# Layer one's short convolution by pairs of heads: interleaved rows in one product, the odd rows placed by a transfer

## The reference, cut to what matters

```python
avg = cumsum(x, axis=1) / arange(1, l + 1)          # l = 1024 tokens, 256 features = 16 heads of 16
ci = avg per head                                   # (b * H, l, 16)
w = softmax(stt_energy + sigmoid(gate) * dyn)       # 31 weights per token and head, from ci @ W_pe
out[t] = sum over kk of w[t, kk] * padded[t + kk]   # a causal window of 31 tokens
v = out (all heads side by side) @ W_fc.T + residual
v = layernorm(v) * gamma + beta
```

## Time and profile before

| | |
|---|---|
| median of 3 runs | 3462.36 us (3459.31 to 3465.0) |
| the profiled execution's own time | 3466.14 us |
| its span, first to last instruction | 3464.3 us |
| mean granted TensorE clock | 0.979 of full speed |
| instructions | 67597 |

### The profile page before, as it was taken

One profiled execution on the slowest core, in us unless ns is written; L12 is line 12 of the kernel. 1 busy time (PEld: TensorE's weight loads), 2 busy tenths in 40 slices (PEclk: granted clock), 3 DMA queues, 4 the chain that ended last, 5 costly groups with the idle time before them and its releaser, 6 DMA issues.

```text
span 3464.3 us, 67597 instructions
## 1 busy us (share of the span) xinstructions
PE 3307.4 (95%) x25168; PEld 2785.4 (80%) x25168; DVE 2606.8 (75%) x6172; ACT 2076.2 (60%) x4055; POOL 1269.7 (37%) x1073
## 2 busy tenths in 40 slices
PE   7999999999996999999999469999999999999999
PEld 4888888888885799999999347888888888888888
DVE  5877887788777865555554578888888888888884
ACT  4677777777765555655665345555555555555554
POOL 1333333332331366666665332333333332322320
PEclk8999999999998999999999689999999999999999
DMA  5332233222212344444444465555655555655541
GB/s 180 102 114 90 93 114 108 80 64 80 75 45 80 87 115 103 96 104 109 105 97 86 86 132 113 113 127 127 129 125 127 120 123 126 130 125 128 128 102 41
DMA packets 746021, 366.38 MB, mean 106 GB/s; under 512 B 551278, under 2 KB 696246, under 8 KB 745558
## 3 DMA queue, kind: packets, MB, share of 16 engines
q1 hardware_dynamic: 717278, 319.57, 36.4%
q0 software_dynamic: 28416, 42.49, 6.6%
HBM read 224.93 MB, written 135.99 MB: 104 GB/s over the span
## 4 chain that ended last, share of the span: by engine, by line
PE 87%; DVE 6%; ACT 2%; DMA 2%; issue 1%; SPq 1%; POOL 1%; POOLq 0%; DVEq 0%; ACTq 0%
PE bank L2294 10%; PE bank L853 10%; PE bank L1612 10%; PE bank L2308 10%; PE bank L1596 10%; PE bank L833 10%; PE bank L2265 7%; PE bank L130 5%; PE bank L810 3%; PE bank L2244 3%; PE bank L2276 3%; PE bank L2239 1%; ACT sides L1140 1%; PE bank L818 1%; PE bank L846 1%
## 5 line engine op out<-in xcount | busy, mean ns | idle before, releaser
L1492 DVE TENSOR_TENSOR hidden_low<-bank,hidden_high 128x512 fp32r<-128x512 f32 x256 | 176.2, 689 | 263.0 <-ACT hidden_high L1193 262.8
L609 ACT ACTIVATE bank<-bank,b 128x512 f32<-128x512 f32 x256 | 172.7, 675 | 282.2 <-PE bank L833 281.9
L1186 ACT ACTIVATE bank<-bank,fc_bias 128x512 f32<-128x512 f32 x256 | 169.5, 662 | 263.5 <-PE bank L1596 263.5
L853 PE MATMUL bank<-w_high,gT_low 128*128 128x256 f32 x1024 | 309.8, 303 | 2.9 <-DVE gT_low L725 2.9
L2052 ACT ACTIVATE bank<-bank,l_b 128x512 f32<-128x512 f32 x256 | 168.9, 660 | 238.8 <-PE bank L2294 238.8
L2308 PE MATMUL bank<-l_w_high,l_hidden_low 128*128 128x256 f32 x1024 | 307.6, 300 | 0.0
L2265 PE MATMUL bank<-bandT,window 128*32 128x96 f32 x5632 | 271.2, 345 | 22.4 <-DMA bandT<-bands 20.2
L853 PE MATMUL bank<-w_low,gT_high 128*128 128x256 f32 x1024 | 289.4, 283 | 0.0
L853 PE MATMUL bank<-w_high,gT_high 128*128 128x256 f32 x1024 | 289.4, 283 | 0.0
L2308 PE MATMUL bank<-l_w_low,l_hidden_high 128*128 128x256 f32 x1024 | 286.0, 279 | 0.0
L2308 PE MATMUL bank<-l_w_high,l_hidden_high 128*128 128x256 f32 x1024 | 285.5, 279 | 0.0
(11 more groups left out here) (372 smaller groups left out, 10709.3 us busy)
## 6 DMA issues: line engine op xcount, KB each, us to landing
bandT<-bands SPq DMA_DIRECT2D x352, 240.0 KB, 3.7
fc_full<-in_L_ffn_fc_wT SPq DMA_DIRECT2D x32, 1024.0 KB, 5.5
bands<-zeros SPq DMA_DIRECT2D x22, 768.0 KB, 8.6
x<-in_L_attn_x SPq DMA_DIRECT2D x32, 512.0 KB, 6.3
moe_output<-zeros SPq DMA_DIRECT2D x32, 512.0 KB, 7.1
x_after_retention<-x SPq DMA_DIRECT2D x32, 512.0 KB, 2.9
moe_input_and_gates<-xn SPq DMA_DIRECT2D x32, 512.0 KB, 7.7
moe<-moe_output SPq DMA_DIRECT2D x32, 512.0 KB, 7.4
```

What stands on the lines that cost most here:

```text
L609: e.activation(bank[:, :], bank[:, :], ACT.Gelu_apprx_tanh, bias=t.b1[:, f:f + 1]).then_inc(s("g_full"), 1)
L853: m = pe.matmul(out, x, w, start=False, stop=f == KF - 1 and j == 2 and c % 2 == 1)
L1492: v.tensor_tensor(t.hidden.low[:, n % SLICES, :], K.banks[t.bank["expand", i, f, 0]][:, :], t.hidden.high[:, n % SLICES, :], ALU.subtract) ...
```

## The change

The bank of a tile now holds the product of each pair's 32 rows with both heads' bands. `window` has no zeros: row 2d of a pair is feature d of the even head, row 2d + 1 that of the odd head. The moving operand is `bandT[:, :, first:first + 2]`, for each token the weights of both heads, which lie side by side; the matmul has 192 columns, token by token, even and odd. Of the result, an even row is wanted at even columns and an odd row at odd ones. ScalarE makes two copies: the odd columns into a new tile `odd` (all rows), and the even columns into `convT` (all rows). Then a DMA issued on ScalarE's queue writes the 64 odd rows of `odd` over the odd rows of `convT`. `mix` waits for these transfers. The rows of `W_fc` are permuted on the host to match. GpSimd's two memsets of `window` go. `PLACES_D`, `STARTS_D` and `BANKS_D` have new numbers throughout and a new step `place_odd`; the length of a batch stays 16 slots.

```diff
 EARLIER = {...,
+           "odd_placed0": ("x_in0", 256), "odd_placed1": ("x_in1", 256)}
...
 PLACES_D = {
-    "kernel_product": (10.8, 12.8, 14.85, 16.8, 18.8, 20.8, 22.79, 24.8), "gated": (10.8, 12.8, 14.61, 16.8, 18.82, 20.8, 22.8, 24.8),
-    "energies": (11.61, 13.56, 15.61, 17.61, 19.47, 21.61, 23.61, 24.94),
-    "add_in": (6.08, 13.95), "l1_low": 1.03,
-    "convolve": (16.82, 18.13, 19.59, 21.03, 22.48, 23.93, 25.38, 26.83, 28.28, 29.73, 31.18),
-    "mix": (19.06, 20.4, 21.9, 24.8, 26.2, 27.7, 30.6, 31.43),
+    "kernel_product": (10.78, 12.89, 14.88, 16.78, 18.79, 20.83, 22.75, 24.72),
+    "gated": (10.69, 12.36, 14.84, 16.4, 18.61, 20.87, 22.64, 24.58),
+    "energies": (11.36, 13.53, 15.74, 17.77, 19.27, 21.4, 23.55, 25.44),
+    "add_in": (5.06, 13.12), "l1_low": 1.09,
+    "convolve": (16.97, 18.07, 19.67, 21.03, 22.22, 23.95, 25.02, 26.9, 28.62, 29.73, 31.18),
+    "place_odd": (17.09, 18.19, 19.9, 21.15, 22.42, 24.02, 25.25, 27.02, 28.74, 29.85, 31.3),
+    "mix": (19.15, 20.61, 22.1, 24.89, 26.55, 27.9, 31.19, 32.35),
...
-    t.window = K.ring(ctx, "window", 2, [P, H // 2, 2, 2 * t.HD])
+    t.window = K.ring(ctx, "window", 2, [P, H // 2, 2 * t.HD])
+    t.odd = K.ring(ctx, "odd_heads", 2, [P, KD, TT])
...
-            e.memset(t.window[0][:, :, :, :], 0.0)
-            e.memset(t.window[1][:, :, :, :], 0.0).then_inc(s("pool_setup"), 1)
...
         elif name == "window_turn":
-            out = bass.AP(all_of.tensor, all_of.offset, [all_of.ap[0], [4 * t.HD, H // 2], [3 * t.HD, 2], [1, t.HD]])
-            e.copy(out, src).then_inc(s("window"), 1)
+            e.copy(t.window[n % 2][:, :, :].rearrange("p a (d q) -> p a q d", q=2),
+                   K.banks[t.bank["window_turn", b, *args, 0]][:, 0:D].rearrange("p (a q d) -> p a q d", q=2, d=t.HD)).then_inc(s("window"), 1)
         elif name == "convolve":
             e.wait_ge(s("conv_product"), n + 1)
+            if n >= 2:
+                e.wait_ge(*K.later(f"odd_placed{n % 2}", 16 * (n // 2)))
+            heads = K.banks[t.bank["convolve", b, i, 0]][:, 0:2 * KD * TT].rearrange("p (k t q) -> p k t q", k=KD, q=2)
+            e.copy(t.odd[n % 2][:, :, 0:size], heads[:, :, 0:size, 1])
             if before:
                 e.wait_ge(s("mixed"), before)
-            e.copy(t.convT[:, :, place:place + size],
-                   K.banks[t.bank["convolve", b, i, 0]][:, 0:KD * TT].rearrange("p (k t) -> p k t", k=KD)[:, :, 0:size]).then_inc(s("convT"), 1)
+            e.copy(t.convT[:, :, place:place + size], heads[:, :, 0:size, 0]).then_inc(s("conv_taken"), 1)
+        elif name == "place_odd":
+            e.wait_ge(s("conv_taken"), n + 1)
+            e.dma_start(t.convT[1::2, :, place:place + size], t.odd[n % 2][1::2, :, 0:size]).then_inc(K.later(f"odd_placed{n % 2}")[0], 16)
...
-                for odd in range(2):
-                    for g in range(4):
-                        pair = 4 * k + g
-                        m = pe.matmul(bank[32 * g:32 * (g + 1), k * TT:(k + 1) * TT], t.window[n % 2][:, pair, odd, :],
-                                      t.bandT[n % 2][:, :, g // 2 * H // 2 + k * t.HR + g % 2 * 2 + odd], start=odd == 0, stop=odd == 1)
+                for g in range(4):
+                    first = g // 2 * H // 2 + k * t.HR + g % 2 * 2
+                    out = bank[32 * g:32 * (g + 1), 2 * k * TT:2 * (k + 1) * TT].rearrange("p (t q) -> p t q", q=2)
+                    m = pe.matmul(out, t.window[n % 2][:, 4 * k + g, :], t.bandT[n % 2][:, :, first:first + 2], start=True, stop=True)
...
         elif name == "mix":
-            pe.wait_ge(s("convT"), NT * b + -(-(ch + 1) * P // TT))
+            last = NT * b + -(-(ch + 1) * P // TT) - 1
+            for n in range(max(last - 1, 0), last + 1):
+                pe.wait_ge(*K.later(f"odd_placed{n % 2}", 16 * (n // 2 + 1)))
...
-    arrays["L1_attn_W_fcT"] = x["L1_attn_W_fc"].T
+    head = D // x["L1_attn_stt_energy"].shape[1]
+    arrays["L1_attn_W_fcT"] = x["L1_attn_W_fc"].T.reshape(-1, 2, head, D).transpose(0, 2, 1, 3).reshape(D, D)
```

More of the change, by code:

```diff
@@ L1642 @@
-    "mix": (19.06, 20.4, 21.9, 24.8, 26.2, 27.7, 30.6, 31.43), "center_mid": (19, 20.4, 21.9, 24.8, 26.21, 27.7, 30.6, 32),
-    "root_mid": (24.98, 32.56), "residual_mid": (25.83, 32.44), "stats_x3": (26.59, 34.51), "root_x3": (27.13, 35.02), "norm_x3": (27.48, 35.68),
-    "turn_mid": (29.71, 36.62), "load_out_row": 35.09, "gain_out": (42.68, 50.91), "result": (45.63, 54.65),
+    "l1_split": 0.56, "l1_low": 1.09, "l1_contract": 2.58, "share": (2.65, 10.18), "load": (0.27, 7.36),
+    "join": (4.53, 13.36), "add_in": (5.06, 13.12), "stats_in": (7.02, 13.73), "root_in": (8.85, 14.8),
@@ new lines @@
+    "norm_in": (8.65, 16.12), "load_bias_row": 4.22, "turn_in": (9.04, 17.18), "average": (9.6, 9.68, 17.83, 18.37),
+    "add_row": (11.51, 19.58), "kernel_product": (10.78, 12.89, 14.88, 16.78, 18.79, 20.83, 22.75, 24.72),
+    "gated": (10.69, 12.36, 14.84, 16.4, 18.61, 20.87, 22.64, 24.58),
+    "energies": (11.36, 13.53, 15.74, 17.77, 19.27, 21.4, 23.55, 25.44),
+    "exponentials": (11.88, 14.39, 16.25, 18.33, 20.29, 22.53, 24.43, 25.87),
+    "softmax": (12.34, 14.56, 16.39, 18.4, 20.53, 22.31, 24.26, 26.3),
@@ L1645 @@
+    "residual_mid": (27.07, 34.6), "stats_x3": (27.09, 35.11), "root_x3": (27.69, 35.78), "norm_x3": (29.71, 36.37),
+    "turn_mid": (30.56, 37.64), "load_out_row": 35.03, "gain_out": (42.39, 50.65), "result": (46.04, 55.68),
 }
@@ L2012, in layer_one_scalar @@
             n = b * NT + args[0]
-            if n == 0:
-                e.wait_ge(*K.setup("pool", "windows"))
             e.wait_ge(s("window_turned"), n + 1)
@@ L2017, in layer_one_scalar @@
                 e.wait_ge(s("conv_product"), n - 1)
-            all_of = t.window[n % 2][:, :, :, :]
-            out = bass.AP(all_of.tensor, all_of.offset, [all_of.ap[0], [4 * t.HD, H // 2], [3 * t.HD, 2], [1, t.HD]])
-            src = K.banks[t.bank["window_turn", b, *args, 0]][:, 0:D].rearrange("p (a e d) -> p a e d", e=2, d=t.HD)
-            e.copy(out, src).then_inc(s("window"), 1)
+            e.copy(t.window[n % 2][:, :, :].rearrange("p a (d q) -> p a q d", q=2),
+                   K.banks[t.bank["window_turn", b, *args, 0]][:, 0:D].rearrange("p (a q d) -> p a q d", q=2, d=t.HD)).then_inc(s("window"), 1)
         elif name == "convolve":
@@ L2259, in layer_one_tensor @@
             pe.wait_ge(s("window"), n + 1)
-            bank = take(t.bank["convolve", b, *args, 0], "convT", n + 1)
+            bank = take(t.bank["convolve", b, *args, 0], "conv_taken", n + 1)
             for k in range(KD):
-                for odd in range(2):
-                    for g in range(4):
-                        pair = 4 * k + g
-                        m = pe.matmul(bank[32 * g:32 * (g + 1), k * TT:(k + 1) * TT], t.window[n % 2][:, pair, odd, :],
-                                      t.bandT[n % 2][:, :, g // 2 * H // 2 + k * t.HR + g % 2 * 2 + odd], start=odd == 0, stop=odd == 1)
+                for g in range(4):
+                    first = g // 2 * H // 2 + k * t.HR + g % 2 * 2
+                    out = bank[32 * g:32 * (g + 1), 2 * k * TT:2 * (k + 1) * TT].rearrange("p (t q) -> p t q", q=2)
+                    m = pe.matmul(out, t.window[n % 2][:, 4 * k + g, :], t.bandT[n % 2][:, :, first:first + 2], start=True, stop=True)
             m.then_inc(s("conv_product"), 1)
```

80 lines of the change are left out of this document (41 added, 39 removed).

## The result

The changed kernel takes 3494.94 us in the median of 4 runs (3491.19 to 3499.62), the kernel before 3461.57 on the same chip: 1.0096 of it, 95% interval 1.0079 to 1.0114. It is 33 us slower, where 75 us less were forecast, and outside the prediction's range.

What follows compares the result with a forecast made beforehand. TensorE was taken as the bound, with VectorE close behind. 105 us saved by products, less 15 for the transfer and 15 for VectorE, gave 75 us: 3391 on the profiled execution, 3387 as median; range 3352 to 3436.

Steps and rivals of the forecast that it cites:

- What a pair of columns costs: Layer one's product on TensorE: a group of 192 paired columns takes 0.165 us, saving 0.66 us a tile, 105 us.
- the pair pays in part: Rival on the product: a group takes 0.25 us, saving 0.32 us per tile; 3431 us, chance 0.12.
- the change doesn't do what it says: Rival on the product: every column pays, a group takes 0.33 us, waits come on top; 3472 us, chance 0.06.
- ScalarE: Second copy 0.31 us and DMA issue up to 0.43 us a tile, at most 8.1 us per batch, hidden by idle time.
- The transfer: Wait of `mix` for the odd rows: 0.5 us late, twice a batch, at second and sixth mixes; 15 us given back.
- I take 2.5: Time in us from the odd-row transfer's issue to its landing, between bounds of 1.7 and 4.2.
- The rival that put the break-even at 3.8 us: Late transfer: waits reach the gain at a 3.8 us landing; at 4.5, 50 us slower, 3512 us, chance 0.06.
- VectorE: Work and remaining waits of 81 us a batch fit TensorE's 82.6; 1 us a batch, 15 us, given back.
- Its work stays 77.9 us per batch: VectorE's busy time in a steady batch of layer one stays unchanged at 77.9 us.
- In the new places it does: VectorE fits TensorE's shorter batch in the new order: most of 6.4 us of waits goes, about 3 us stay.
- VectorE becomes the bound: Rival: VectorE's waits stay in other places, a batch takes 87.9 us; 30 us won, 3432 us, chance 0.12.
- The slower side: Outcome that the changed kernel is slower, by the late transfer and the rest: chance 0.10.

Runs made afterwards that it cites:

- f1: e1 with the fifth chunk's `energies` at 19.3 instead of 19.27, behind an `l1_low` on VectorE; odd rows not placed: 3399.98 us, 0.9812 of the kernel before.
- e1: a1 with the first `residual_mid` of a batch moved from 27.07 to 26.5; odd rows not placed: 3430.13 us, 0.9906 of the kernel before.
- a1: The changed kernel without its transfer (odd rows not placed), with the new tables: 3447.69 us, 0.9949 of the kernel before.
- d1: The changed kernel with its transfer sent to rows nobody reads, and `mix` not waiting for it (the very last excepted): 3447.62 us, 0.9954 of the kernel before.
- a2: The changed kernel without its transfer (odd rows not placed), with the tables of before: 3442.61 us, 0.9935 of the kernel before.

## Why the prediction was wrong

The ledger, from the runs: the products were to shorten TensorE's path by 105 us, from 3462 to 3357, and its busy time in f1 bears that out (7.1 us less a batch, 15 batches). f1 is at 3400, so 43 us go to waits other than those below. The subtraction ahead of `l1_low` costs 30 (e1 to f1), the residual passes 18 (a1 to e1), the transfer 47 (change to a1): 3495. Each item is idle time and the clock that goes with it.

- *What a pair of columns costs*: right. 0.62 us are saved per tile, 0.66 forecast. The rivals "the pair pays in part" and "the change doesn't do what it says" are out. Two columns side by side do give the full rate here. The rule of the Trainium skill that the prediction weighed (SBUF — State Buffer, section "Door 1: The DMA port swizzle") says so of two hits per line, and the trace agrees, with groups of 192 such columns 0.165 us apart.
- *ScalarE*: right. It is busy for 54.4 us of 91.9 per batch, 52.5 before (the prediction has 52.3); the issue takes 0.60 us on its queue, not 0.43, and hides (d1). Its order was not looked at: steps between copy and issue made two transfers per batch 1.9 us late.
- *The transfer*: the term was mis-sized, 47 us for 15. The mechanism was partly right: of TensorE's idle time ahead of mixes, 3.3 us a batch, 1.9 lie before the fifth, 1.0 before the second, 0.3 before the eighth and 0.2 before the sixth, where the second and the sixth had been taken for the tight ones. The fifth's last tile is one of the two that are issued late. The step that failed is the landing, "I take 2.5": there is no one landing. It is 1.9 with the DMA engines free and mostly 4 to 5 when they are full, and the tightest mixes depend on tiles of the second kind. The rival that put the break-even at 3.8 us had the mechanism, but counted on 6.3 us of gain a batch to be eaten first. The rule of the Trainium skill on pieces under 512 bytes (DMA: Bandwidth & Descriptors, "Specifications") played no part that shows: pieces of 384 bytes land in 1.9 us on free engines, under the 2.5 assumed, though no run has larger ones to compare. Another section of the same page ("Why small descriptors are slow (HBM only)") says that transfers from SBUF to SBUF don't suffer the penalty of small ones.
- *VectorE*: the step that failed most. "Its work stays 77.9 us per batch" took busy time as a property of the instructions. It went to 81.3, since the new order puts VectorE's residual passes beside GpSimd's additions. And "In the new places it does" (fit) looked at one wait, GpSimd's energies, which did fall as forecast; what the places do to `l1_low`, on which TensorE waits, was not sorted out. Where 15 us were given back, 89 were lost: the 105 less the 16 that a1 wins on the kernel before beside it. Of these 89, 48 are taken back by moving two steps on VectorE (a1 to f1). The rival "VectorE becomes the bound", 3432, gives the time of the change without its transfer within 16 us (3448), though not by the mechanism it named, the unchanged waits of VectorE; that one shows in a2, where the old tables keep them.
- *The clock*: the sum had no term for it. Beside its longer waits TensorE was also granted less, and its busy time a batch is 84.4 us in the change against 82.4 in f1. These 2 us are part of the items above and not further ones.
- *The slower side*: it took both failures. Without the transfer's wait the change is at 3448; with the transfer, but with the two passes and the issue in better places, at 3439; both are under the time before.

What stays open is how much of the 43 us in f1 can be won. TensorE idles 3.0 us a batch there, where it idled 0.5 before; 1.7 of it lies ahead of `kernel_product` and ends with VectorE, as shown above, the rest is in waits of 0.4 us a batch or less. No run removes them.

## What to carry to other kernels

When an order of steps is changed, VectorE's busy time may change with it: list its passes that read two operands from SBUF, and look which of GpSimd's instructions run beside them, before and after; the view of waits doesn't show the loss, durations by line (median against maximum) do. A new transfer on the path is costed by what the DMA engines carry at that moment, by the distance in the list from the copy to its issue, and for each waiting step by itself. Shifting a waiting step later on one engine moves the wait to whoever comes behind it on the next. And a wait of TensorE can cost more than its length, since the granted clock falls beside it: compare TensorE's busy time, too.

## What was not expected of the hardware

A transfer of 49 KB from SBUF to SBUF in 128 pieces of 384 bytes takes 1.9 us with the DMA engines at a share of 0.15 and 4.7 us at 1.12 (shares count a packet whole in the window in which it starts, so they can pass 1). Its issue holds ScalarE's queue for 0.60 us, SyncE's issue of `bandT` 0.43. A VectorE pass of 478 ns takes 1.48 or 2.60 us beside a GpSimd instruction of 1.44 or 2.56 us, the full length of the other. A small pass with a single tensor input stretches as well: `l_less_mean_x` (128 x 4) takes 170 ns before, on average 465 after, and 1.93 us beside a GpSimd addition of 2.39 us in f1. With TensorE idle for 7.5 us a batch its granted clock is 0.98, and the same matmuls keep it busy for 84.4 us, where it is 82.4 at a clock of 1.00.
